# Node logits of a graph-attention kernel: one 48-column product per slot instead of three 16-column ones, and row transfers of three batches

## What is computed

```python
h = (x @ W).reshape(n, heads, out_ch)
a_src = jnp.sum(h * att_src[None], axis=-1)
a_dst = jnp.sum(h * att_dst[None], axis=-1)
e = jax.nn.leaky_relu(a_src[src] + a_dst[dst], NEG_SLOPE)
m = jax.lax.stop_gradient(jax.ops.segment_max(e, dst, num_segments=n))
p = jnp.exp(e - m[dst])
denom = jax.ops.segment_sum(p, dst, num_segments=n)
out = jax.ops.segment_sum(h[src] * (p / denom[dst])[..., None], dst, num_segments=n)
```

## Time and profile before

| | us |
|---|---|
| runs without profile | 3773.42, 3755.59, 3769.68 (median 3769.68) |
| the profiled execution | 3798.44 |
| its span | 3796.7 |
| PE busy over the span | 2719.0 (72%) |
| DVE busy | 2286.5 (60%) |
| POOL busy | 1816.9 (48%) |
| granted TensorE clock over the span | 0.839 of full speed |

### The profile page before, as it was taken

One profiled execution on the slowest core, in us unless ns is written; L12 is line 12 of the kernel. 1 busy time (PEld: TensorE's weight loads), 2 busy tenths in 40 slices (PEclk: granted clock), 3 DMA queues, 4 the chain that ended last, 5 costly groups with the idle time before them and its releaser, 6 DMA issues. The chain is left out here.

```text
span 3796.7 us, 66505 instructions
## 1 busy us (share of the span) xinstructions
PE 2719.0 (72%) x14765; PEld 2077.4 (55%) x14766; DVE 2286.5 (60%) x6866; ACT 1182.9 (31%) x4644; POOL 1816.9 (48%) x1892
## 2 busy tenths in 40 slices
PE   8577767677766776785666666666666666699998
PEld 6455555555555555574555544455444444557666
DVE  6766766666766766784555544445655565635445
ACT  5533333333333333332122111122222321343342
POOL 0355555555555555502555555666555554501111
PEclk9788998888888888897788878777777777599999
DMA  5566666666666666513444464544333333321220
GB/s 190 150 180 174 182 185 180 173 180 182 181 174 181 182 181 178 165 37 95 122 136 137 123 180 116 153 127 106 100 97 100 101 103 97 134 86 52 78 86 12
DMA packets 272861, 512.09 MB, mean 135 GB/s; under 512 B 53920, under 2 KB 176779, under 8 KB 272658
## 3 DMA queue, kind: packets, MB, share of 16 engines
q0 software_dynamic: 118128, 361.70, 34.2%
q1 hardware_dynamic: 140006, 134.66, 12.8%
q10 hardware_dynamic: 14524, 13.40, 1.0%
HBM read 463.94 MB, written 49.57 MB: 135 GB/s over the span
## 5 line engine op out<-in xcount | busy, mean ns | idle before, releaser
L921 PE MATMUL PS<-w_G,w_S 128*128 128x260 f32 x3520 | 982.0, 435 | 356.5 <-DVE ACC L1011 228.7
L1318 POOL DMA_INDIRECT weights<-table,w_idx x880 | 845.0, 960 | 727.3 <-issue 293.7
L808 POOL DMA_INDIRECT w_G<-table,w_idx x880 | 847.1, 963 | 677.4 <-issue 286.0
L921 PEld LDWEIGHTS PS<-w_G,w_S 128*128 128x128 f32 x3520 | 726.1, 215 | 531.3 <-issue 258.6
L1505 PE MATMUL PS<-weights 128*128 128x257 f32 x1760 | 648.4, 513 | 353.0 <-DVE ACC L1697 215.7
L1505 PEld LDWEIGHTS PS<-weights 128*128 128x128 f32 x1760 | 407.3, 253 | 480.6 <-issue 286.0
L999 DVE TENSOR_TENSOR w_G<-w_G,PS 128x512 f32<-128x512 f32 x660 | 432.4, 683 | 64.5 <-ACT PS L831 33.9
L844 ACT ACTIVATE w_G<-w_G 128x64 f32<-128x64 f32 x1760 | 443.9, 335 | 0.2
L1011 DVE TENSOR_TENSOR ACC<-ACC,PS 128x520 f32 x464 | 321.2, 692 | 183.9 <-PE PS L921 90.6
L1340 ACT ACTIVATE w_PW<-w_Z 128x4 f32<-128x4 f32 x220 | 45.3, 206 | 1091.8 <-DVE w_Z L1682 841.6
L1697 DVE TENSOR_TENSOR ACC<-ACC,PS 128x257 f32 x464 | 196.3, 423 | 279.5 <-issue 181.5
(11 more groups left out here) (322 smaller groups left out, 3321.2 us busy)
## 6 DMA issues: line engine op xcount, KB each, us to landing
w_DR<-rows SPq DMA_DIRECT2D x220, 128.0 KB
weights<-rows SPq DMA_DIRECT2D x220, 128.0 KB
weights<-in_L_ffn_w SPq DMA_DIRECT2D x16, 1024.0 KB, 7.7
w_G<-table,w_idx POOLq DMA_INDIRECT x880
weights<-table,w_idx POOLq DMA_INDIRECT x880
table<-ACC SPq DMA_DIRECT2D x49, 260.0 KB
xbuf<-XR SPq DMA_DIRECT2D x8, 1040.0 KB
XR<-xbuf SPq DMA_DIRECT2D x7, 1040.0 KB, 5.3
```

The lines of the kernel that those rows point to most:

```text
L808: pool.indirect_dma_start(G[:, r, b, :], None, table, IndexOn(ap=idx[:, r, b:b + 1], axis=0)).then_inc(fetched[r], 16)
L921: last = pe.matmul(PS[:, 2 * j + a, 0:W // layer.banks], lhsT, rhs, start=b == slots[0], stop=b == slots[-1])
L1318: pool.indirect_dma_start(G[:, r, b, :], None, table, IndexOn(ap=idx[:, r, b:b + 1], axis=0)).then_inc(fetched[r], 16)
```

## The change

In walk one the three parts of a node lie side by side (`parts` is [tile, part, 16] instead of [part, tile, 16]), so that one product of 48 columns a slot replaces three of 16. PSUM then holds the three parts, and a new DVE reduction adds them into `node` in SBUF; the two later readers of PSUM read `node`. The own semaphore counts four links a batch instead of three. The second half of `one_hot` moves ahead of the subtraction, and nothing stands between the subtraction and the cap. In both walks SP transfers the lanes of three batches at once (384 KB), into one of two halves, instead of one batch into one of three places. To fit it in, `diag` of the wide path (not taken here) moves into `S`; in walk two `DR`, `ST`, `q`, `YC` and `YT` change places, and `YC`, `YT` share memory with `HS`, which is done with by then.

```diff
-        DR = sb(tag + "DR", [P, AHEAD, B * P], BF16)
+        DR = sb(tag + "DR", [P, 2, CHUNK, B * P], BF16)
-        parts = sb(tag + "parts", [P, 3, TILES, 2 * H], BF16)
+        parts = sb(tag + "parts", [P, TILES, 3, 2 * H], BF16)
+        node = sb(tag + "node", [P, 2, B, 2 * H])
...
-            for n in range(NB):
-                if n >= AHEAD:
-                    sp.wait_ge(st_ready, n - AHEAD + 1)
-                sp.dma_start(DR[:, n % AHEAD, :], rows16[n * B:(n + 1) * B, :].rearrange("b e -> (b e)").partition_broadcast(P)).then_inc(row_in[n % AHEAD], 16)
+            for c in range(-(-NB // CHUNK)):
+                if c > 1:
+                    sp.wait_ge(st_ready, (c - 1) * CHUNK)
+                w = min(CHUNK, NB - c * CHUNK)
+                sp.dma_start(DR[:, c % 2, 0:w, :].rearrange("p n e -> p (n e)"),
+                             rows16[c * CHUNK * B:(c * CHUNK + w) * B, :].rearrange("b e -> (b e)").partition_broadcast(P)).then_inc(row_in[c % 2], 16)
...
-                        for i in range(3):
-                            last = pe.matmul(PS[:, 6 + r % 2, b * 2 * H:(b + 1) * 2 * H], ST[:, r % 2, b, :],
-                                             parts[:, i, bass.ds(at, 1), :].rearrange("p a b -> p (a b)"), start=i == 0, stop=i == 2)
+                        last = pe.matmul(PS[:, 6 + r % 2, b * 6 * H:(b + 1) * 6 * H], ST[:, r % 2, b, :],
+                                         parts[:, bass.ds(at, 1), :, :].rearrange("p a i b -> p (a i b)"), start=True, stop=True)
...
-                node = PS[:, 6 + r % 2, 0:B * 2 * H].rearrange("p (b c) -> p b c", b=B)
+                dve.tensor_reduce(node[:, r % 2, :, :], PS[:, 6 + r % 2, 0:B * 6 * H].rearrange("p (b i c) -> p b c i", b=B, i=3), X, ALU.add).then_inc(own, 1)
+                between(0)
+                dve.wait_ge(own, 4 * n + 1)
...
                 dve.tensor_tensor(z4, a_src, a_dst, ALU.add).then_inc(own, 1)
-                between(0)
-                dve.wait_ge(own, 3 * n + 1)
+                between(1)
+                dve.wait_ge(own, 4 * n + 2)
                 dve.scalar_tensor_tensor(z, z, SLOPE, z, ALU.mult, ALU.max).then_inc(own, 1)
-                between(1)
-                dve.wait_ge(own, 3 * n + 2)
-                dve.tensor_tensor(z, z, node[:, :, H:2 * H], ALU.subtract).then_inc(own, 1)
                 between(2)
-                dve.wait_ge(own, 3 * n + 3)
+                dve.wait_ge(own, 4 * n + 3)
+                dve.tensor_tensor(z, z, node[:, r % 2, :, H:2 * H], ALU.subtract).then_inc(own, 1)
+                dve.wait_ge(own, 4 * n + 4)
```

More of the change, by code:

```diff
@@ L722, in walk @@
     RING = 6
-    AHEAD = 3
+    CHUNK = 3
     assert SLOTS % B == 0
@@ L741, in walk @@
         hot = sem(tag + "hot")
-        row_in, st_ready = [sem(f"{tag}row_in{r}") for r in range(AHEAD)], sem(tag + "st_ready")
+        row_in, st_ready = [sem(f"{tag}row_in{u}") for u in range(2)], sem(tag + "st_ready")
         spread = sem(tag + "spread")
@@ L766, in walk @@
         XS = place("x" + tag + "Sx", [P, P])
[L767 to L769 removed]
+        off = sb("x" + tag + "off", [P, P])
+        diag = S[:, 4:6, :, :].rearrange("p r b q -> p (r b) q")
         self_ready, own_scaled = sem(tag + "self_ready"), sem(tag + "own_scaled")
@@ L1096, in _ @@
             split_ = Chain(dve, split)
[L1097 to L1101 removed]
+            split_.link(dve.tensor_copy(parts[:, :, 0, :], ADM[:, :, :]))
+            split_.link(dve.tensor_tensor(rest[:, :, :], ADM[:, :, :], parts[:, :, 0, :], ALU.subtract))
+            split_.link(dve.tensor_copy(parts[:, :, 1, :], rest[:, :, :]))
+            split_.link(dve.tensor_tensor(rest[:, :, :], rest[:, :, :], parts[:, :, 1, :], ALU.subtract))
+            dve.tensor_copy(parts[:, :, 2, :], rest[:, :, :]).then_inc(parts_ready, 1)
             turned_hot(At(None, RING, 0))
@@ L1160, in walk2 @@
         SW = place("w1_SW", [P, 2, B, P])
-        DR = place("w1_DR", [P, AHEAD, B * P // 2]).bitcast(BF16)
+        DR = sb("w1_DR", [P, 2, CHUNK, B * P], BF16)
         HS = place("w1_HS", [P, 2, ROW2])
         idx = sb("w1_idx", [P, RING, B], I32)
-        ST = sb("w1_ST", [P, 2, B, P], BF16)
+        ST = place("w1_ST", [P, 2, B, P // 2]).bitcast(BF16)
+        q = place("w1_q", [P, 2, QK])
         parts = sb("w1_parts", [P, 3, TILES, 2], BF16)
@@ L1169, in walk2 @@
         fetched = [sem(f"w1_fetched{r}") for r in range(RING)]
-        row_in = [sem(f"w1_row_in{r}") for r in range(AHEAD)]
+        row_in = [sem(f"w1_row_in{u}") for u in range(2)]
         staged, st_ready, spread, z_ready, weighed, scaled, summed, merged, own, split, parts_ready, released = (
@@ L1204, in walk2 @@
         gp, nkm, ks = early("gp", [P, 2]), early("nkm", [P, 1]), early("ks", [P, 1])
-        YC = sb("YC", [P, D])
-        YT = sb("YTC", [P, 2, P])
+        after_mine = HS[:, :, :].rearrange("p u c -> p (u c)")
+        YC = after_mine[:, 0:D]
+        YT = after_mine[:, D:2 * D].rearrange("p (k q) -> p k q", k=2)
         WQ = sb("WQ", [P, 2, QK])
-        q = sb("q", [P, 2, QK])
         QT = sb("QT", [P, P])
@@ L1285, in raw_rows, with chunk @@
                     sp.dma_start(XR[0:LAST, TILES - 1, 0:D], x[(TILES - 1) * P:N, :]).then_inc(xc_in[6], 16)
-            def row(n):
-                if n >= AHEAD:
-                    sp.wait_ge(st_ready, n - AHEAD + 1)
-                sp.dma_start(DR[:, n % AHEAD, :], rows16[n * B:(n + 1) * B, :].rearrange("b e -> (b e)").partition_broadcast(P)).then_inc(row_in[n % AHEAD], 16)
+            def chunk(c):
+                if c > 1:
+                    sp.wait_ge(st_ready, (c - 1) * CHUNK)
+                w = min(CHUNK, NB - c * CHUNK)
+                sp.dma_start(DR[:, c % 2, 0:w, :].rearrange("p n e -> p (n e)"),
+                             rows16[c * CHUNK * B:(c * CHUNK + w) * B, :].rearrange("b e -> (b e)").partition_broadcast(P)).then_inc(row_in[c % 2], 16)
             for n in range(NB):
-                row(n)
+                if n % CHUNK == 0:
+                    chunk(n // CHUNK)
                 if n == 2:
```

21 lines of the change are left out of this document (9 added, 12 removed).

## The result

The changed kernel takes 3746.77 us (median of 16 runs, 3739.31 to 3773.87), the kernel before 3767.14 us beside it (16 runs): ratio 0.9955, 95% interval 0.994 to 0.9969. That is 20 us less, where +5 was forecast. The profiled span is 3748.6 us; that of before (3796.7) came from an execution some 30 us above its median, so the 48 us between the two profiles overstate the change. Of these 48, 12 lie between the first and the last gather of walk one (1473 and 1461 us) and 30 in walk two (1437 and 1407 us), where only the transfers and the places in SBUF had changed.

The account below looks back on a forecast made before the run. PE signals reaching POOL's gather loop late were taken to set the pace, no engine being full. -4 - 5 + 14 + 0 = +5 us on the 3769.7 us median gave 3775; own range 3755 to 3790, 8 in 10 3715 to 3820.

Parts of the forecast that it names:

- What bounds the kernel: Both walks: no engine is full; POOL's four gathers a batch wait for late PE signals, 6.64 us a batch in walk one.
- held groups: Walk one: 96 of 175 gather groups start late although PE's sum had ended long before, its signal arriving late.
- half of DVE's +86: Walk one: rival in which DVE's longer chain costs half of +86 us, giving 3810 us; chance 0.03.
- Part 1, PE's products: Walk one, PE: four products for twelve, 0.25 us for 0.52 a batch, worth -4 and -5 us.
- The term for timely groups: Walk one: in 11 of 175 groups started right after PE's sum, with PE on the path, 0.29 us saved: -4 us.
- the second effect: Walk one: some of 9 late-signal groups start without a gap once sums end 0.29 us earlier; half of 10: -5 us.
- Part 2, the reduction: Walk one, DVE: reduction +0.27 and reorder +0.12 us a batch, on the path in 36 of 220 batches: +14 us.
- Part 3, the transfers: Both walks, SP: same bytes in a third of the transfers, still hidden; zero, bounds -5 to +5 us.
- The clock rival: Walk one: less PE work lowers PE's granted clock below 0.83, slowing the sums; 3812 us, chance 0.18.
- The DVE rival: Walk one: DVE paces each batch, so +0.39 us counts 220 times, +86, 3856 us; chance 0.07.
- The rival of fewer late signals: Lateness comes from many small products in PE's queue, so a fifth of the waiting goes: 3717 us, chance 0.17.
- The range: Whole kernel: 8 in 10 between 3715 and 3820 us, taking in 3812 and 3717 but not the ends of 0.07.

Follow-up runs that it names:

- e8: The kernel before, unchanged, run again for its profile; it took 3802.22 us (23 runs) in that sitting.
- m1: Changed kernel without the reduction, two small parts left out of the logits, against the kernel before: 3767.72 against 3801.02 us, ratio 0.9916.
- e5: The whole changed kernel run again, against the kernel before at 3802.22 us: ratio 0.9942, -22 us.
- e7: Kernel before plus the 48-column product and the reduction, transfers of one batch kept, against the kernel before at 3802.22 us: ratio 0.998, -8 us.
- h1: Changed kernel with DVE's chain of logit steps shortened by algebra, against the kernel before at 3101.61 us: 3104.86 us, ratio 1.0014.
- e6: Kernel before plus transfers of three batches in both walks, old product, against the kernel before at 3802.22 us: ratio 0.9988, -5 us.
- e1: Kernel before plus transfers of three batches in both walks, old product, against the kernel before at 3103.94 us: 3102.79 us, ratio 0.9997.
- e2: Kernel before plus the 48-column product and the reduction, old transfers, against the kernel before at 3103.94 us: 3154.86 us, ratio 1.0175.
- g2: Changed kernel with each 48-column product issued three times, against the kernel before at 3101.61 us: 3157.11 us, ratio 1.0191.
- n1: Changed kernel with DVE's chain of logit steps shortened by algebra, run in another sitting against the kernel before: ratio 1.0038.

## Why the prediction was wrong

**What bounds the kernel** held: the loop of late signals sets the pace in a late sitting, and all counts of groups came out again in e8 (40, 94, 41). Three of its figures are off without effect on the sum: the 2.2 us of idle time before held groups is the mean, the median being 1.95; 64 us are 6% of PE's 1057, not 4% (measured 37 us, 1056.7 to 1019.7); and half of DVE's +86 gives 3813, not 3810.

**Part 1, PE's products,** is the step that failed. The price, 0.25 us for four products, held at full clock (twelve took 0.45 us there, four take 0.26 in 104 of 140 batches of the profile after), and the saving came out smaller than forecast, 0.23 us for 0.29, since 0.25 is a price at full clock and the 0.52 it was taken from is a mean over both. The worth was -4 - 5 = -9 us. Measured: m1's -0.84% less the transfers' -0.12%, -27 us (20 to 35). The term for timely groups, -4, was not measured by itself; the mis-sized one is the second effect, held groups that become gapless, put at -5 where about -23 are left for it. It counted 9 candidates of 175 by the edge that the groups of before had (sum ended by 2.72 us after the previous start), took half and 0.9 us net each. 14 became gapless, since the edge was not a fixed moment: 36 groups in e8 whose sum ended 2.9 to 4.5 us after the start of a group that was not gapless itself had to wait, 7 in m1. And a converted group gave more than 0.9: from e8 to m1 a batch is 0.135 us shorter, 30 us over 220, or 1.7 us for each of the 14 x 220 / 175 = 17.6, since the timely batches became shorter as well (7.61 to 7.37 us). Taking "held" as a cost that only counts who is near its edge today was the error. With the reduction beside it a converted group gives less: 11 more from e8 to e5 and a batch 0.04 us shorter. Why the edge moved stays open.

**Part 2, the reduction,** held in its prices: 351 ns for 354, 0.26 us in the chain for 0.27, 0.22 for the step to the cap, 5.11 us a batch for 5.08. Its +14 us stand between the +10 (0 to 20) from e5 and the +20 from e7. That they come by the timely groups that it was worked out from is not shown, since m1 without a reduction has as many when they are counted to 1.3 us.
The Trainium skill, page "VectorE: DVE Perf Modes", section "Rules for kernel authors", calls the reduction the slowest operation of DVE and advises another form on a hot path. The rows here don't show it slower: a reduction of 256 elements took 420 ns, a comparison of 256 (L957) as much, and the 351 ns for 192 lie below. And h1, which keeps it and saves elsewhere in the chain, takes its cost in a prompt sitting from 51 to 4 us.

**Part 3, the transfers,** 0 with bounds of -5 to +5: -5 (-0.4 to -8) in the late sitting, nothing in the prompt one. Walk two, the only place where they stand alone, runs from its first to its last group in 1432 us in e8 and 1430 in e5. In the record's own pair of profiles, though, it is 30 us shorter after, where "unchanged within 10 us" was forecast. No experiment reproduces that: e6 has 1434.6 us for e8's 1435.8, first to last gather. So it isn't the transfers' as far as these runs go; its cause stays open.

**The clock rival** is out: the granted clock of walk one is 0.88 of full speed after, 0.87 before. In prompt sittings it is 0.96 to 0.99 (from 400 to 1200 us); PE is busy there for 83% of the time from 140 to 1250 us in e1 and 75% in e2, against 71% of walk one before.

**The DVE rival** was given 0.07, with the condition that it decides once the held signals vanish, and +86 us. The condition was right and its likelihood was asked of the wrong thing: not the change removes the held signals, the sitting does. There, +51 us. The size was off because POOL's batch is 5.09 us and not DVE's old 4.69: only what DVE has above POOL counts, 0.06 us a plain batch, and the twelve with four sums.

**The rival of fewer late signals** put the lateness on the many small products. With a third of them DVE's two "remote" waits add up to 57.8 + 111.7 = 169.5 us against 198.5 (131.0 + 67.5), and to 236.0 in m1, where DVE has no new work: the lateness isn't less. The 29 us less of the whole change are below the 63 that DVE got to do in addition (150 x 0.42). By the semaphore's records (last section) a quarter of the sums' signals come at least 2.7 us late in e8, 3.4 in e5 and 4.0 in m1. The rival's mechanism falls.

**The range** of 8 in 10 (3715 to 3820) held the time; the forecast's own (3755 to 3790) didn't, the sign of the forecast was wrong, and by the interval the gain is 0.3 to 0.6%. Of the 25 us between +5 and -20, 18 are part 1's and 5 part 3's. That the wide range held is in part luck: its low end was set by the rival of fewer late signals, whose mechanism fell.

## What to carry to other kernels

When the pace is set by signals that are held back while an engine issues DMAs, 0.2 us off a step is worth nothing or, for single batches, over 3 us of waiting (3.6 in e8), by the side of the edge on which the step ends: make a histogram of where in the group the step ends, not only of who waits today. Keep each engine's batch below that of the engine that would pace the loop without the delays (here DVE's 5.15 us against POOL's 5.09, though in the walk of the late sitting DVE looked idle 30% and POOL 44% of the time), because the delays may be gone elsewhere. And measure both kinds of sitting before a change of 1% is believed: the whole change gives -0.5 and -0.6% in late ones, and e2 and g2, which stand for it, +1.75% and +1.9% in a prompt one, where the change itself was not run.

## What the chip showed that was not expected

The same program takes 3802 or 3104 us. The gathers are not the reason: their packets of 4160 bytes took 232 ns on average in e8 (late) and 230 in e1 (prompt), and the whole gather queue 34.1% of 3798.9 us and 41.4% of 3099.0, 1295 and 1283 us. What differs is when PE's signals arrive: in e1 the record of the semaphore's change follows the recorded end of PE's sums by 0.01 us in at least three quarters of 352 cases; in e8 by 0.7 us in the median and 2.7 us at three quarters (some changes have no record there, so the upper figure takes in some of the next). It can be neither the program nor the chip, since one chip took 3801 us for the kernel before in m1's sitting and 3103 in n1's. What makes a sitting late stays open.
The Trainium skill, page "Perfetto Trace Analysis", section "Tensor Engine Instruction (MATMUL, LD_WEIGHTS)", says that a matmul's recorded end is an estimate and that the signal is pushed and propagated behind it. The traces agree that the two differ, by 0.01 us in e1 and by up to several us in e8; that the latter depends on the sitting is what these runs add.
